# Fifth batch also in seven block products, late chunks spread over four batches, three x sums of a batch by accumulating transfers

## What is computed

```python
ae = layernorm(cond, ln_g, ln_b)
xw = gelu(ae @ w1 + b1) @ w2 + b2              # per batch: A and B, each 512 x 8
layer = base_layer + A @ B.T                   # 512 x 512, one per batch
x = x + (x + x @ layer)                        # first layer
ys = cond / sqrt(512); d = rsqrt((ys*ys) @ (weight*weight) + 1e-8)
x = x + ((x * ys) @ weight) * d                # second layer
```

## Time and profile before

| | before |
|---|---|
| median of three runs | 288.04 us |
| profiled execution: time / span | 287.95 / 286.2 us |
| granted TensorE clock, mean | 0.999 |
| TensorE busy | 281.4 us (98%) |
| VectorE / ScalarE busy | 228.1 us (80%) / 170.1 us (59%) |
| GpSimd busy | 18.6 us (6%) |

### The profile page before, as it was taken

How to read it: one execution, slowest core, us unless ns; L and a number is a source line. 1 busy time by engine, 2 the same in 40 slices (tenths; PEclk the granted TensorE clock), 3 DMA queues, 4 the chain that set the end, 5 groups by cost and what they waited for, 6 DMA issues and landing times.

```text
span 286.2 us, 3812 instructions
## 1 busy us (share of the span) xinstructions
PE 281.4 (98%) x1368; PEld 222.0 (78%) x1368; DVE 228.1 (80%) x341; ACT 170.1 (59%) x260; POOL 18.6 (6%) x35
## 2 busy tenths in 40 slices
PE   8999999999999999999999999999999999999994
PEld 8778374756788888888888888888888888888783
DVE  3979969936688999984899978766787998987972
ACT  4757865530653648863648865534785587743771
POOL 5000000000520211000211000020000000000000
PEclk9999999999999999999999999999999999999999
DMA  6999797978044113499313499201134152371105
GB/s 187 372 425 422 290 421 297 419 302 324 2 147 147 76 74 128 165 279 407 123 79 142 149 301 419 89 0 74 73 114 182 74 179 116 101 266 73 53 23 220
DMA packets 13697, 55.31 MB, mean 193 GB/s; under 512 B 1776, under 2 KB 1776, under 8 KB 11376
## 3 DMA queue, kind: packets, MB, share of 16 engines
q1 hardware_dynamic: 10800, 45.64, 42.7%
q10 hardware_dynamic: 2880, 9.44, 8.3%
HBM read 38.30 MB, written 16.78 MB: 192 GB/s over the span
## 4 chain that ended last, share of the span: by engine, by line
PE 98%; DVE 0%; issue 0%; POOL 0%; POOLq 0%
PE tile L1495 33%; PE tile L1464 23%; PE tile L1384 7%; PE aux L1323 6%; PE acc L1255 5%; PE tile L1287 4%; PE tile L1270 4%; PE tile L1430 4%; PE spare L1323 3%; PE acc L1323 3%; PE tile L1226 2%; PE aux L1309 1%; PE aux L1233 1%; PE aux L1400 1%; PE spare L1309 1%; PE acc L1309 1%
## 5 line engine op out<-in xcount | busy, mean ns | idle before, releaser
L1495 PE MATMUL tile<-xs,qs 128*128 128x512 f32 x420 | 97.4, 390 | 0.0
L1495 PEld LDWEIGHTS tile<-xs,qs 128*128 128x128 f32 x420 | 78.7, 188 | 17.0 <-issue 0.7
L1464 PE MATMUL tile<-xs,qs 128*128 128x512 f32 x288 | 68.2, 389 | 0.0
L1464 PEld LDWEIGHTS tile<-xs,qs 128*128 128x128 f32 x288 | 54.1, 188 | 11.2
L1000 DVE TENSOR_TENSOR xs<-stream,xs 128x1024 fp32r<-128x1024 f32 x33 | 40.0, 1221 | 10.3 <-ACT xs L537 10.0
L537 ACT CAST xs<-stream 128x1024 fp32r<-128x1024 f32 x33 | 34.3, 1049 | 4.3 <-ACT stream L591 1.9
L606 ACT ACTIVATE stream<-tile,dts 128x512 f32<-128x512 f32 x40 | 26.6, 687 | 12.3 <-PE tile L1495 12.1
L591 ACT ACTIVATE stream<-tile,dts 128x512 f32<-128x512 f32 x24 | 16.4, 688 | 27.9 <-PE tile L1464 27.9
L1069 DVE TENSOR_TENSOR qs<-base,qs 128x512 fp32r<-128x512 f32 x38 | 25.0, 685 | 4.1 <-ACT qs L566 4.1
L1105 DVE SCALAR_TENSOR_TENSOR stream<-tile,dts,stream 128x512 f32<-128x512 f32 x30 | 21.9, 747 | 6.1 <-PE tile L1495 4.3
L417 POOL TENSOR_SCALAR amk<-asq,mask 128x512 fp32r<-128x512 f32 x8 | 14.3, 1794 | 172.9 <-PE spare L1309 98.9
(11 more groups left out here) (170 smaller groups left out, 324.2 us busy)
## 6 DMA issues: line engine op xcount, KB each, us to landing
stream<-in_w2u SPq DMA_DIRECT2D x12, 1024.0 KB, 10.0
stream<-in_xT SPq DMA_DIRECT2D x21, 512.0 KB, 5.6
out<-stream ACTq DMA_DIRECT2D x17, 512.0 KB, 2.6
out<-stream SPq DMA_DIRECT2D x14, 512.0 KB, 2.8
xr<-in_xT SPq DMA_DIRECT2D x11, 512.0 KB, 4.2
xr<-in_w2u SPq DMA_DIRECT2D x2, 1024.0 KB, 15.6
base<-in_w2u SPq DMA_DIRECT2D x2, 1024.0 KB, 10.4
w1s<-in_w1n SPq DMA_DIRECT2D x4, 256.0 KB, 5.7
```

The costliest lines, as they stand in the source:

```text
L1464: last = nc.tensor.matmul(tiles[o][:], q_slot(b, cc)[:, u, cols], x_slot(b, (h, cc // 2))[:, v, cc % 2], start=cc == 0 and (u, v) == (0, 0 ...
L1495: last = nc.tensor.matmul(tiles[bank + m][:], q_slot(b, q)[:, u, cols], x_slot(b, x)[:, v, k], start=opens and k == 0 and (u, v) == (0, 0) ...
```

## The change

1. Batch 4 joins `FAST`; `plain_batch` serves 0 and 2 alone, and its branches for late batches go.
2. The twelve late chunks are placed one by one (`LATE_AT`): batch 5's after j4, j5, j6 of batch 3 and j0 of batch 4; batch 6's after j4, j5, j6 of batch 4 and j0 of batch 5; batch 7's after j5, j6 of batch 5 and j0, j1 of batch 6. The building of `rs` moves ahead with them, and its scaling from VectorE (`r_scale`) to ScalarE (`r_scaled_ahead`).
3. t3, t1 and t4 are made by GpSimd transfers that add into a raw buffer (`accum_op`), the first two with a quarter of x from HBM, the third with the sum in SBUF. Only t2 stays on VectorE (`x_sum`). Signs change with it (the product of this blocking with b12 negated): two q sums become scalar_tensor_tensor, and `dts_neg` scales three of the blocks.
4. Raw buffers are handed out by name instead of in turn; loads go out as (1,0), (0,0), (0,1), (1,1) for a fast batch. Orders within ScalarE's and VectorE's lists shift.

```diff
-FAST = (1, 3, 5, 6, 7)
+FAST = (1, 3, 4, 5, 6, 7)
-LATE_STEP = {6: 1, 7: 3}
+LATE_AT = {(3, 4): (5, 0), (3, 5): (5, 1), (3, 6): (5, 2), (4, 0): (5, 3), (4, 4): (6, 0), (4, 5): (6, 1),
+           (4, 6): (6, 2), (5, 0): (6, 3), (5, 5): (7, 0), (5, 6): (7, 1), (6, 0): (7, 2), (6, 1): (7, 3)}
...
+            if b in FAST:
+                b12, b11, b21, t2, b22, left = comes_free
+                homes = {(1, 0): b12, (0, 0): b11, (0, 1): b21, "sum": t2, (1, 1): b22}
+                comes_free = [left, b12, b11, t2, b22, b21]
...
+                quarters = X_LOADS[b not in FAST]
                 if b - 2 in FAST and b - 1 in FAST:
                     store_block(b - 2, "c21", 1)
+                load_x(b, *quarters[0])
+                load_x(b, *quarters[1])
                 if b - 1 in FAST:
                     store_block(b - 1, "c11", 0)
+                elif b - 2 in FAST:
                     store_block(b - 2, "c21", 1)
+                load_x(b, *quarters[2])
+                load_x(b, *quarters[3])
                 if b - 1 in FAST:
                     store_block(b - 1, "c22", 2)
...
+            def add_t3(b):
+                raw_loaded(pool, b, (1, 0))
+                nc.gpsimd.dma_start(x_raw(b, (1, 0)), xT[b, 1, 1], accum_op=ALU.add).then_inc(t3_added, 16)
+            def add_t1(b):
+                pool.wait_ge(x_lo, x_op[b, "b11"] + 1)
+                pool.wait_ge(x_stepped, FAST.index(b) + 1)
+                nc.gpsimd.dma_start(x_raw(b, (0, 0)), xT[b, 1, 0], accum_op=ALU.add).then_inc(t1_added, 16)
+            def add_t4(b):
+                pool.wait_ge(x_lo, x_op[b, "b21"] + 1)
+                pool.wait_ge(x_stepped, FAST.index(b) + 1)
+                nc.gpsimd.dma_start(x_raw(b, (0, 1)), x_raw(b, "sum"), accum_op=ALU.add).then_inc(t4_added, 16)
...
+            masked(0)
+            masked(1)
+            masked(2)
+            add_t3(1)
+            masked(3)
+            add_t1(1)
+            add_t4(1)
+            masked(4)
+            add_t3(3)
+            masked(5)
+            add_t1(3)
+            add_t4(3)
+            masked(6)
...
+            def r_scaled_ahead(b, kc):
+                act.wait_ge(r_lo, NO[b] * KC + kc + 1 - RTMP)
+                nc.scalar.activation(rtmp[:, kc % RTMP], w1s[:, kc], ACT.Copy,
+                                     scale=ys[:, b, kc:kc + 1]).then_inc(r_scaled, 1)
...
+            r_scaled_ahead(STORED, 0)
+            r_scaled_ahead(STORED, 1)
             act.wait_ge(c_done, 1)
...
+            nc.vector.tensor_scalar(dts_neg[:], dts[:], -1.0, None, ALU.mult).then_inc(dts_turned, 1)
+            def x_sum(b):
+                if raw_after[b, "sum"]:
+                    dve.wait_ge(x_lo, raw_after[b, "sum"])
+                raw_loaded(dve, b, (0, 0))
+                dve.wait_ge(t3_added, 16 * (FAST.index(b) + 1))
+                nc.vector.tensor_tensor(x_raw(b, "sum"), x_raw(b, (1, 0)), x_raw(b, (0, 0)),
+                                        ALU.add).then_inc(x_stepped, 1)
```

More of the change, by code:

```diff
@@ L418, in _ @@
                                         ALU.mult).then_inc(amk_ready, 1)
+            pool.wait_ge(mask_ready, 1)
+            masked(0)
[11 more added lines that the diff above has]
+            masked(6)
+            add_t3(4)
+            add_t1(4)
+            add_t4(4)
+            add_t3(5)
+            masked(7)
+            add_t1(5)
+            add_t4(5)
+            add_t3(6)
+            add_t1(6)
+            add_t4(6)
+            add_t3(7)
+            add_t1(7)
+            add_t4(7)
         @block.scalar
@@ L616, in plain_batch @@
                 n = b + 1
-                late = STORED <= n < B
-                early_r = n in FAST and STORED <= n + 1 < B
                 x_high(b, (1, 0))
+                if b > 0:
+                    r_high(NO[STORED], 0)
+                    r_high(NO[STORED], 1)
                 evacuate_out(b, 0, 0)
                 x_high(b, (1, 1))
-                if late:
-                    r_high(NO[n], 0)
-                    r_high(NO[n], 1)
+                if b > 0:
+                    r_scaled_ahead(STORED, 2)
+                    r_scaled_ahead(STORED, 3)
@@ L659, in plain_batch @@
-                if early_r:
-                    r_high(NO[n + 1], 0)
+                q_high(n, "a11")
+                q_high(n, "a12")
+                x_high(n, "b11")
+                evacuate_out(b, 1, 0)
+                x_high(n, "b21")
+                evacuate_out(b, 1, 1)
+                q_high(n, "s2")
+                q_high(n, "s3")
                 evacuate_out(b, 1, 2)
-                if early_r:
-                    r_high(NO[n + 1], 1)
-                    r_high(NO[n + 1], 2)
-                    r_high(NO[n + 1], 3)
@@ new lines, in fast_batch @@
+                q_high(b, "a22")
+                keep_late(b, 0)
+                if late:
+                    r_high(NO[late], 0)
+                    r_high(NO[late], 1)
+                x_high(b, "t1")
+                keep_late(b, 1)
+                if late:
+                    r_scaled_ahead(late, 2)
+                    r_scaled_ahead(late, 3)
+                if b == B - 2:
+                    q_high(n, "a11")
+                    q_high(n, "a12")
+                x_high(b, "b22")
+                evacuate_block(b, "b", 2, 1, 1)
@@ new lines, in fast_batch @@
+                if late:
+                    r_high(NO[late], 2)
+                    r_high(NO[late], 3)
+                x_high(b, "t4")
+                if n not in FAST:
+                    if n < B:
+                        q_high(n, 0)
+                        q_high(n, 1)
+                    evacuate_block(b, "c", 4, 2, 1)
+                    if n < B:
+                        x_high(n, (0, 0))
+                        q_high(n, 2)
+                        q_high(n, 3)
+                        x_high(n, (0, 1))
@@ L1140, in fast_pair @@
+                for cc in range(KC):
+                    p_sum(n, cc)
+                q_sums_first(n)
+                q_low(n, "a11")
+                q_low(n, "a12")
+                q_sums_last(n)
+                x_low(n, "b11")
+                x_low(n, "b21")
+                x_sum(n)
+                q_low(n, "s2")
+                q_low(n, "s3")
+                for cc in range(KC):
+                    p_sum(n + 1, cc)
             def fast_pair(b):
                 n = b + 1
-                a11, a12, a21, a22 = [q_raw(n, k) for k in ((0, 0), (0, 1), (1, 0), (1, 1))]
@@ L1155, in fast_pair @@
-                x_low(n, "b21")
-                x_sums_last(n)
-                if LATE_STEP[n] > 1:
+                x_low(n, "b11")
+                x_sum(n)
+                if b < B - 2:
+                    q_sums_first(n)
+                finish_block(b, "c22", 3, "c", 2, 1)
+                x_low(n, "b21")
+                if b < B - 2:
+                    q_low(n, "a12")
+                    q_sums_last(n)
+                if (b, 5) in LATE_AT:
+                    x_low(n, "t2")
+                    q_low(n, "s2")
+                    q_low(n, "s3")
+                    q_low(n, "s1")
+                    finish_block(b, "c21", 6, "b", 1, 1)
+                else:
```

352 lines of the change are left out of this document (117 added, 235 removed).

## The result

| | before | after |
|---|---|---|
| median (range) | 288.08 us (287.32 to 288.23, four runs) | 284.62 us (283.99 to 285.36, four runs) |
| profiled execution: time / span | 287.95 / 286.2 us | 285.36 / 283.5 us |
| TensorE, first product of batch 0 starts | 82.62 | 83.20 |
| batch 3's start to TensorE's end | 148.81 to 282.56: 133.75 | 149.39 to 280.27: **130.88** |

The ratio after to before is 0.9886, 95% interval 0.9857 to 0.9916: faster, by about 1.1%. The forecast was 285.1 with a range of 284.4 to 287.4.

The account below looks back on a forecast made before the run. TensorE was taken as the bound. Batch 4's matmuls (2.72) and batch 7's late start (0.47) gave 3.15 us less, tight places 0.25 back: 287.95 - 3.15 + 0.25 = 285.05, so 285.1 us, range 284.4 to 287.4.

Parts of the forecast that it names:

- TensorE bounds, so matmuls removed are time gained: TensorE busy 281.4 of 286.2 us; batch 4 in seven products removes 2.72 us, if the other lists still deliver.
- 0.25 for tight places: Batch 5 on VectorE and ScalarE: 0.1 us charged for c22, 0.15 for three deadlines with 0 to 0.4 to spare.
- Batch 7's late start: Batch 7 took 19.51 us, not 19.04; its last chunk, moved after j1 of batch 6, gives back 0.47.
- The tightest place: Batch 5, where j1 to j5 run without a chunk's relief; deadlines met with 0 to 0.4 us to spare.
- the walk: Step-by-step schedule of batch 5 on TensorE, VectorE and ScalarE, starting at 207.54, with each operation's ready and due times.
- The load of b11 in batch 5: SyncE issues it at 217.9, ScalarE copies at 221.8; 3.7 us taken, 4.1 before TensorE waits: no stall.
- Rival (b): b11 lands late in batch 5: a 7 us load costs 2.9, giving 288.0 us; chance 0.09.
- VectorE's account: VectorE needs 23.5 us in batches 4 and 5, which last 30.84 and 27.89: enough, so order is the question.
- The adding transfers: GpSimd's adds for t1, t3, t4: 5 us each, bounded 3.0 to 10.0; cost nothing; sign: land in 4 to 7.
- rival (a): Slow adds become the wait in batches 1, 3 and 7 above 8.4 us each; at 9, 292 us; chance 0.09.
- (c): VectorE's and ScalarE's lists run later than reckoned in batch 5, likely 1 to 2 us: 286.6; chance 0.14.
- (d): Batch 7 does not recover and still loses about 0.5 us: 285.5, within the forecast's range; no separate chance.

Follow-up runs that it names:

- the two runs that take the stall before j5 away and leave c22 where it is: Changed kernel with batch 7's first chunk after j4 of batch 5: 285.37 us; changed kernel with half of part c evacuated before b11's copy in batch 5: 284.92 us.
- the one with fourteen fills: Changed kernel with GpSimd idling through fourteen fills of an idle tile (8.2 us) ahead of each t1 adding transfer: 299.92 us, ratio 1.0390.

## Why the prediction was right, point by point

**TensorE bounds, so matmuls removed are time gained.** Right. Twelve more cost 2.82 us where I had worked out 2.72 for twelve fewer.

**Sum.** From batch 3's start on I had 3.15 us less and 0.25 for tight places, 2.90 in all; measured were 2.87. That they agree to 0.03 is partly luck, as the 0.25 stood at other places (below). The profiled execution came out at 285.36 against 285.05. Of these 0.3 us the first product, which started 0.58 later than before, accounts for more than all; 0.11 more lie outside the span. Against them stands the tail behind TensorE's last matmul, which I had called the same work: it took 3.64 us before and takes 3.23 now, and no run shows why. The medians fell by 3.46 us, more than the 3.15 that the sum has without any stall. That surplus is not TensorE's: the shorter tail and the scatter of the start-up are large enough for it, but the medians can't be taken apart.

**Batch 7's late start, 0.47.** The size was right: batch 7 takes its steps of 2.72. The reason was half of it. I put the whole down to the place of the chunk; the runs showed that this alone makes it 1.14 us worse, and that VectorE's order (sums and a12 ahead of c21) is the other half. The change has both, but my reasoning went by the first alone, so that the whole 0.47 came back is partly luck.

**The tightest place.** Right place, batch 5 from j4 to j6. Batch 5 began 0.56 us later than in the walk (208.10 instead of 207.54). Shifted by that, ScalarE's copy of t4 starts when the walk had it (220.3, measured 220.86), and c22's first half, which starts at 229.24 and takes 0.70, ends when it had that (229.4, measured 229.94). Of the 0.25 us charged, the two terms changed places. c22 was charged 0.1: it is 0.09, but only in the two runs that take the stall before j5 away and leave c22 where it is. In after the stall before j5 gives c22 more time, and it costs nothing. The 0.15 for the other deadlines turned into 0.31, by the step after this one.

**The load of b11 in batch 5.** This is the term that was mis-sized. I took 3.7 us and "no stall", from the row of the same stretch, where the median of all was 4.4. It took 4.2, from 218.72 to 222.92, and it was issued 0.26 later than the walk had it (217.9 and the shift are 218.46). Of the 4.1 us that I had before TensorE waits, 3.84 were left, and 4.2 less 3.84 is 0.36 where 0.31 were measured. The mechanism, the copy of b11 with part c queued behind it, was named. With the median in place of the picked row the sum would have had 0.3 for it, though by two errors that cancel: 4.4 is 0.2 more than it took, and the issue was 0.26 later than in the walk. Rival (b) is the same mechanism at a larger size.

**VectorE's account.** I had 23.5 us in each of batches 4 and 5. The windows cut at TensorE's batches show 23.4 and 20.9:

```profile
177.27:208.10 30.83, 30.83 (x138) 25.53 (x137) 23.39 (x33) 22.77 (x34) 4.18 (x4) 1.00 0.65 175
208.10:236.00 27.90, 27.84 (x123) 22.76 (x123) 20.90 (x29) 20.84 (x31) 2.57 (x3) 1.00 0.68 192
```

In batch 5 four of the 33 instructions fall outside: the first two eyes run at 207.05, ahead of TensorE's start, and the two halves of c21 at 236.56, behind its end. With them (0.6 and 1.4 us) it is 22.9. The account holds to some 0.6 us.

**The adding transfers.** I took 5 us within 3.0 and 10.0. Measured are 5.5 and 5.8 in the median from HBM, and 6.7 to 7.6 from SBUF, the slowest 9.3. The bounds held, the value taken was too low, and of the sign "4 to 7 us" six of the eighteen transfers fell outside. t4 took 7.6 us in batch 1 and 9.3 in batch 7, above the 7.1 and 8.0 that I had allowed. It changed nothing, for two reasons. They had the slack, and more than 3.5 us of it. And t1 and t4 don't run one after the other: GpSimd issued those of batch 1 at 103.60 and 104.20, they took 5.4 and 7.6 us, so both had landed 8.2 us after the first was issued; in series they would have needed 13.0. My margins of 7.1 to 8.4 us each, reckoned for one after the other, were therefore too strict, and the threshold of rival (a) with them. The estimate of 3.2 us that I had worked out from the Trainium skill, DMA: Bandwidth & Descriptors (Anatomy of one DMA), is not what the trace shows for an adding transfer: all of them took longer. By the Trainium skill, Collectives: The Full Stack (The bandwidth ceiling), an add needs two source reads, which agrees with the trace in direction, 5.5 and 5.8 us from HBM beside plain loads into the same buffers of 5.1 and 4.1; why those from SBUF take longer no run here separates.

**GpSimd beside VectorE.** The trace has no transfer held back by VectorE: an issue is shown with 0.86 to 1.22 us on GpSimd and comes right after its release. In the direction of rival (a) nothing was found.

**Rivals.** (a) needs a delay between 3.5 and 8.2 us that isn't there. (b) happened at a tenth of its size (0.31 of 2.9 us) and (c) at less (0.09, and only once (b) is mended), in the places named. (d) didn't happen; moving the chunk alone, in the kernel before, made it happen and worse (1.14 us).

## What to carry to other kernels

Filler work on the engine that bounds (a late chunk here) is two things at once: something others wait for, and the cover under which everything queued elsewhere finishes. Before moving it, list both; the same move lost 1.1 us or won 0.4 depending on one order in VectorE's list. When work is taken off the bounding engine, look for the next engine's relief in the same edit: here three additions a batch became adding transfers that cost TensorE nothing, and put back on VectorE, in the place tried, they cost 4.3 us, more than the twelve matmuls had gained. And an in-order list that copies a freshly loaded buffer ahead of an evacuation should be priced at the median of such loads, not at one picked row.

## What was not expected of the hardware

- **Start-up scatter.** The first product of batch 0 began between 81.96 and 84.91 us in fourteen profiled executions (twelve of them by 83.26), with all but the same instructions ahead of it; why, no run shows. From there to batch 3's start thirteen of them took 66.18 or 66.19 us, all but the one with fourteen fills. A difference of a few tenths of a us has to be read from a stretch of the trace, not from the medians.
- **A late adding transfer hits others first.** Delayed by 3.5 us, the adding transfers met their own deadlines, but a plain load beside them took 7.9 us instead of the 5.1 in after, and batch 3 was 0.86 us longer for it.
- **A long wait costs twice.** In the run with fourteen fills TensorE stood idle for 2.36 and 2.60 us in two places, the granted clock behind each fell to 0.50, and the twelve matmuls that followed took 4.56 and 4.42 us instead of 2.72.
- **Stores.** SyncE's stores went from 2.8 to 5.0 us in the median, and are at 2.9 in the run without the adding transfers. In batch 7 of after ScalarE even waited for one, the row below from its timeline, with 1.4 us to spare before TensorE would have noticed.

```profile
269.56 1.27 ACT L675 ACTIVATE stream<-tile,dts 128x512 f32<-128x512 f32 x2 [1.02 <-DMA out<-stream]
```
